# Causal attention with a row-maximum pass ahead: where the maxima's matmuls stand in each step

## The reference, cut to what matters

```
scores = jnp.einsum('bqhd,bkhd->bhqk', q, k) / jnp.sqrt(hd)
scores = jnp.where(causal, scores, -1e9)
a = jax.nn.softmax(scores, axis=-1)
out = jnp.einsum('bhqk,bkhd->bqhd', a, v).reshape(B, S, D)
```

## Time and profile before

| | us |
|---|---|
| median of 3 runs | 3145.0 (3141.05 to 3147.88) |
| profiled execution, its own time | 3123.49 |
| its span | 3122.0 |
| phase 2 in it, from the first to the last matmul | 464.9 to 2041.9 |

### The profile page before, as it was taken

How to read it: one execution, slowest core, us unless ns; L and a number is a source line. 1 busy time by engine, 2 the same in 40 slices (tenths; PEclk the granted TensorE clock), 3 DMA queues, 4 the chain that set the end, 5 groups by cost and what they waited for, 6 DMA issues and landing times. The chain is left out here.

```text
span 3122.0 us, 60368 instructions
## 1 busy us (share of the span) xinstructions
PE 2562.5 (82%) x21392; PEld 1316.3 (42%) x21392; DVE 2338.2 (75%) x3780; ACT 1543.6 (49%) x2314; POOL 2254.1 (72%) x1225
## 2 busy tenths in 40 slices
PE   7959978999999999999999999847749888999600
PEld 4524433333333333333333332236638777777500
DVE  4437758888888889888988888015657999999344
ACT  2212216677777777677777677722214444444200
POOL 4433339898889989889899998927737566566376
PEclk9979999999999999999999999968769999999855
DMA  6995542122323233232332321148667666667686
GB/s 193 200 298 180 180 162 74 46 75 81 87 55 83 79 87 86 56 80 81 86 79 63 82 72 41 30 153 254 223 198 224 202 204 205 206 205 206 215 255 198
DMA packets 346973, 435.67 MB, mean 140 GB/s; under 512 B 40858, under 2 KB 276860, under 8 KB 346748
## 3 DMA queue, kind: packets, MB, share of 16 engines
q1 hardware_dynamic: 300796, 350.81, 39.2%
q0 software_dynamic: 17920, 54.55, 5.3%
q10 hardware_dynamic: 28032, 27.27, 2.5%
HBM read 273.43 MB, written 158.47 MB: 138 GB/s over the span
## 5 line engine op out<-in xcount | busy, mean ns | idle before, releaser
L988 DVE TENSOR_REDUCE p_piece_max<-p_ring 128x1 f32<-128x512 f32 (+3 forms) x2160 | 1281.5, 653 | 180.0 <-PE p_ring L1090 97.5
L1046 ACT ACTIVATE p_probs<-p_st 128x1024 f32<-128x1024 f32 (+3 forms) x1280 | 1076.6, 894 | 445.1 <-PE p_st L1122 239.3
L1122 PE MATMUL p_st<-unit_q,unit_k 64*128 64x512 bf16 (+3 forms) x3520 | 417.9, 348 | 22.3 <-POOL p_minus_one L875 11.7
L1140 PE MATMUL p_pv<-p_probs,unit_vg 128*32 128x512 f32 (+3 forms) x3520 | 412.0, 545 | 0.0
L1749 POOL TENSOR_TENSOR p_pv<-p_pr,p_qkv 128x4096 f32<-128x4096 f32 x32 | 347.5, 10860 | 37.4 <-ACT p_pr L1847 36.8
L917 POOL TENSOR_TENSOR p_terms<-p_head_p,p_head_in 128x4096 f32<-128x4096 f32 x32 | 347.6, 10861 | 0.4
L1090 PE MATMUL p_ring<-unit_k,unit_q 64*128 64x512 bf16 (+3 forms) x1600 | 272.8, 354 | 70.1 <-DVE p_piece_max L988 69.8
L1920 PE MATMUL p_y_ps<-p_w,p_hid 128*128 128x256 f32 x1152 | 282.6, 402 | 27.6 <-ACT p_hid L1860 27.6
L896 POOL TENSOR_TENSOR p_terms<-p_head_in 128x4096 f32<-128x4096 f32 x32 | 283.0, 8843 | 8.2 <-POOL p_head_s L904 4.4
L1907 PE MATMUL p_hid_ps<-p_rT,p_w 128*128 128x256 f32 x1152 | 263.8, 382 | 2.9 <-issue 2.6
L923 POOL TENSOR_TENSOR p_terms<-p_terms 128x2048 f32<-128x2048 f32 (+2 forms) x96 | 252.6, 2632 | 17.4 <-POOL p_terms L923 11.7
(11 more groups left out here) (194 smaller groups left out, 3588.3 us busy)
## 6 DMA issues: line engine op xcount, KB each, us to landing
p_w<-ffn_w SPq DMA_DIRECT2D x144, 512.0 KB, 5.1
qk_parts<-p_parts SPq DMA_DIRECT2D x64, 384.0 KB, 3.2
head_qkv<-p_heads SPq DMA_DIRECT2D x16, 1536.0 KB, 6.7
p_rows<-sorted_rows SPq DMA_DIRECT2D x72, 256.0 KB, 4.1
expert_rows<-p_y ACTq DMA_DIRECT2D x72, 256.0 KB, 5.5
unit_q<-qk_parts SPq DMA_DIRECT2D x132, 128.0 KB, 3.2
unit_k<-qk_parts SPq DMA_DIRECT2D x132, 128.0 KB, 3.6
p_x<-attn_x SPq DMA_DIRECT2D x32, 512.0 KB, 6.9
```

The source lines that it names most:

```text
L988: nc.vector.tensor_reduce(piece_max[:, n % 2, h:h + heads, i, pc], ring_ps[g % RING][:, 0:heads * width].rearrange("p (h k) -> p h k", h=h ...
L1046: nc.scalar.activation(probs[:, 2 * turn_of(s, i) + u, :, 0:width], st_ps[u][:, :, 0:width], ACT.Exp).then_inc(probs_done, 1)
L1122: last = nc.tensor.matmul(st_ps[u][:, half, 0:width], k6[s][rows, PAIR * second + u, kt * P:(kt + 1) * P], q6[s][rows, PAIR * second + u, ...
L1140: last = nc.tensor.matmul(pv_ps[hh * VW:(hh + 1) * VW, skip:CT], vg[s][:, kt, hh * VW:(hh + 1) * VW], probs[:, 2 * turn_of(s, i) + hh % PA ...
```

## The change

`ISSUED` is no longer computed from costs. Two tables, one for unit 0 and one for all others, give three bits for each of the 40 steps. Each bit is a place in the step: behind the first `scores`, behind the second, and behind `values`. A place holds at most one pair. Unit 0 still issues 82 pairs and the others 72; the sum by step differs. VectorE's order of reductions is the same as before, apart from which of them stand ahead of its few other instructions at steps 10, 12 and 14.

```
-    def issued(n, i):
-        share = STEPS_BY[i]
-        work = share / END if n == 0 and share < END else n + 1 - END + share
-        whole = int(work + 1e-9)
-        return min(TOTAL, N_PAIR * whole + sum(by <= work - whole + 1e-9 for by in PAIRS_BY))
-    ISSUED = [[issued(n, i) for i in range(N_STEP)] for n in range(UNITS)]
+    FIRST_UNIT = """
+        101 001 011 101 010 011 011 011 111 011 011 110 100 110 100 111 011 111 111 011
+        011 111 011 011 110 101 011 111 011 101 111 011 111 011 001 011 011 011 011 001"""
+    OTHER_UNITS = """
+        100 100 010 101 011 010 011 011 011 111 011 010 011 010 010 111 011 011 011 011
+        011 011 011 011 010 101 011 011 011 011 011 011 011 011 011 011 011 010 101 001"""
+    SPOTS = [[[int(k) for k in step] for step in unit.split()] for unit in (FIRST_UNIT, OTHER_UNITS)]
+    for n in range(UNITS):
+        for i in range(N_STEP):
+            count = ISSUED[n][i] = min(TOTAL, count + sum(spots_of(n)[i]))
...
             def body(n, s):
                 for i in range(N_STEP):
+                    done = before_step(n, i)
+                    ends = [min(TOTAL, done + sum(spots_of(n)[i][:k + 1])) for k in range(3)]
                     scores(n, s, i, 0)
+                    maxima(done, ends[0])
                     scores(n, s, i, 1)
-                    done, upto = before_step(n, i), ISSUED[n][i]
-                    cut = done + (upto - done + 1) // 2
-                    maxima(done, cut)
+                    maxima(ends[0], ends[1])
                     if i >= LAG:
                         values(n, s, i - LAG)
-                    maxima(cut, upto)
+                    maxima(ends[1], ends[2])
```

More of the change, by code:

```diff
@@ L684, in phase2_attend, with spots_of @@
     LAG = 2
-    AHEAD = 6
     TOTAL = N_PAIR * (UNITS - 1)
[L688 to L693, removed]
-    def issued(n, i):
-        share = STEPS_BY[i]
-        work = share / END if n == 0 and share < END else n + 1 - END + share
-        whole = int(work + 1e-9)
-        return min(TOTAL, N_PAIR * whole + sum(by <= work - whole + 1e-9 for by in PAIRS_BY))
-    ISSUED = [[issued(n, i) for i in range(N_STEP)] for n in range(UNITS)]
-    assert all(ISSUED[n][N_STEP - AHEAD - 1] == N_PAIR * (n + 1) for n in range(UNITS - 1))
+    FIRST_UNIT = """
[5 more added lines that the diff above has]
+    SPOTS = [[[int(k) for k in step] for step in unit.split()] for unit in (FIRST_UNIT, OTHER_UNITS)]
+    assert all(len(unit) == N_STEP for unit in SPOTS)
+    def spots_of(n):
+        return SPOTS[1 if n else 0]
+    ISSUED = [[0] * N_STEP for _ in range(UNITS)]
+    count = 0
+    for n in range(UNITS):
+        for i in range(N_STEP):
+            count = ISSUED[n][i] = min(TOTAL, count + sum(spots_of(n)[i]))
+    assert all(ISSUED[n][N_STEP - 7] >= N_PAIR * (n + 1) for n in range(UNITS - 1))
     NEGATED_AT = [min(N_PAIR * u + 1, TOTAL) for u in range(1, UNITS)]
```

## The result

| | before | after |
|---|---|---|
| median of the timed runs, us | 3146.4 (3141.1 to 3149.5, 4 runs) | 3121.5 (3121.0 to 3124.7, 4 runs) |
| after / before | | 0.9925, 95% interval 0.9907 to 0.9942 |
| profiled execution: its time, its span | 3123.5, 3122.0 | 3121.0, 3119.4 |
| phase 2, from the first scores to GpSimd's first instruction of phase 3 | 465.0 to 2053.8 | 465.2 to 2031.6 |
| what lies behind it | 1068.2 | 1087.8 |

The account below looks back on a forecast made before the run. TensorE and VectorE were taken to set 98.0 us a unit, with GpSimd next at 96.5. From a median of 3145, gains of 24.0 over fourteen intervals and 2.7 from unit 0 to unit 1 gave 3118, range 3109 to 3137.

Parts of the forecast that it names:

- The first: Phase 2, fourteen intervals between GpSimd's shifts from unit 1 to 15: 1376.4 us become 1352.4, a gain of 24.0.
- The second: GpSimd's interval from unit 0 to unit 1: 103.7 us become 101.0, a gain of 2.7 (8.1 to −2.4).
- The pace of 96.5: Plain units of phase 2: GpSimd's list becomes the limit at 96.5 us, taken as 96.6 with the handshake.
- The ledger: TensorE and VectorE's loop in a plain unit: 98.0 − 4.1 − 0.4 + 0.1 = 93.6 us, taken as 94.
- the ceiling of 96: TensorE and VectorE's loop in a plain unit: at most 96 or so, if VectorE enters steps 9 to 13 behind.
- the idle time of 5.4 us given to VectorE: From unit 0 to unit 1: 5.4 us of VectorE idle added to 95.6 for 79 pairs, giving 101.0.
- the stated bound of 106.1: From unit 0 to unit 1: upper bound on the interval, 103.7 us plus two more pairs at 1.21 each.
- the cost that the prediction priced for plain units: TensorE's matmuls behind a wait for GpSimd run at half clock, about 2 us a unit, covered within 96.5.
- VectorE waiting at step 14 in each unit: VectorE's head maximum at step 14 waits for GpSimd's head scores, asked for 2.5 us early, in every unit.
- TensorE and VectorE still setting the pace: Rival, chance 0.20: short distances chain, the loop takes 97.2 us a unit, gain 15.4, time 3129.6.
- The step from the old code's three slower units to none: Units 3, 8 and 13, slowed by the clock, raise the average interval to 98.3 us; forecast 96.6 for all fourteen.
- the rival with no gain: Rival, chance 0.10: waits spread over more places are as long in sum; 3145 us, within 3.

Follow-up runs that it names:

- kernel with the tables alone: Changed kernel with new tables for unit 0 (35 pairs before step 14) and for the other units, GpSimd's list left whole; 3114.8 against 3147.8 (0.9902).
- the first experiment: Kernel before with its old count of pairs in each step, but at most one pair at a place; 3114.6 against 3127.7 (0.9952).
- both single edits: Changed kernel with only other tables (3114.8), or with only between-head sums moved to VectorE and unit 0's 33 pairs before step 14 (3108.5); each against 3147.8.
- the two together: Changed kernel with other tables, 35 pairs before step 14 in unit 0, and between-head sums and reciprocals moved from GpSimd to VectorE; 3049.5 against 3126.4 (0.9762).
- the old code with the shorter GpSimd list: Kernel before with GpSimd's reciprocal by pow replaced by a multiply, leaving out the between-head division; one run, 3120.3 us.
- the counts alone: Kernel before with the new tables' count of pairs in each step, in the two old places; 3124.2 against 3127.7 (0.9987).

## Why the prediction was right, point by point

- **The end of it.** Forecast 3118, measured 3121.5; gain 27 forecast, 24.9 measured (phase 2 ends 22.2 us earlier by the traces). The forecast came from two terms, 24.0 and 2.7. The first was right: from the second shift of unit 1 to that of unit 15 it was 1350.9 us (614.3 to 1965.2) against 1352.4 forecast and 1376.3 before, a gain of 25.4. The second had the wrong sign: −2.9. The 21.5 us between the timed runs and the trace of before, which the prediction carried over, are about the distance between the two groups (3147.8 against 3126.4 for the same kernel).
- **The pace of 96.5.** Right, in each plain unit, and GpSimd's waits vanished from them. What was wrong is the room beside it. The ledger gave the loop of TensorE and VectorE as 93.6 us and counted pairs alone; measured without GpSimd it is 96.2, just above the ceiling of 96 too. That the forecast of 96.5 held nevertheless is luck as far as the margin goes: GpSimd's list was still the longer by 0.3 us. The term that the ledger lacked is ScalarE. Steps 0, 1, 5 and 13, with one pair each, hold 1.2 to 1.6 us of TensorE's work (an estimate from its starts in the earlier trace rows), but two full exponentials take 1.94, and in steps 5 and 13 the copy of the finished block adds 0.59; halving its work there gave 94.2. The distances between pairs were priced well in sum: 93.6 against 94.2.
- **Unit 0 into unit 1.** The step that failed is the idle time of 5.4 us given to VectorE. In the stretch from 508.3 to 614.9 it was busy for 95.8 us, as worked out (95.6), but idle for 10.8; the 106.6 us lie above the stated bound of 106.1. Before, it was idle for 10.5 there (103.7 less 93.2 busy); the prediction halved this without a row that shows it, and it stayed. The new table reaches step 14 of unit 0 with two pairs fewer and earlier, waits 6.6 us for GpSimd's first head scores, and has 2.6 us more of reductions behind it. A second cost comes from the longer wait: four matmuls of scores took 1.04 us right behind it, 0.61 in the kernel before. The kernel before:

```profile
509.41 0.61 PE L1122 MATMUL p_st<-unit_q,unit_k 64*128 64x512 bf16 x4 [0.69 <-ACT p_probs L1046]
```

and the changed one:

```profile
509.05 1.04 PE L1125 MATMUL p_st<-unit_q,unit_k 64*128 64x512 bf16 x4 [6.81 <-ACT p_probs L1049]
```

The granted clock of the stretch is 0.98 where it was 1.00: the cost that the prediction priced for plain units fell due here. Unit 0 as before gave 103.3, with more pairs ahead 96.5, both at 1.00. How the 10.8 us divide between the clock and the small waits is open.

- **VectorE waiting at step 14 in each unit** didn't come; in units 1 to 14 the head maxima find GpSimd's scores ready. It is ScalarE's `head_probs` that waits for the shift, 0.2 us. With so little waiting, the clock's cost behind a long wait, put at 2 us, didn't come either in plain units: granted clock 1.00. The kernel with the tables alone shows that it would have come in some units, and that GpSimd's list would have covered it, as the prediction said.
- **The rivals.** TensorE and VectorE still setting the pace was the nearest: 0.3 us in place of 2.5 kept it from being true. The step from the old code's three slower units to none held: no unit from 1 to 13 shows a lower clock, and the longest wait at the ring in unit 5 is 0.45 us. The prediction put the lower clock down to the wait of 1.13 us alone (“only for the longest wait”); but in unit 3 of the kernel before it came twice, the first time behind a wait of 0.80 at 778.7 us, and with single pairs at a place it came in two units behind a wait of 0.70. That waits which are only spread out stay as long in sum, the rival with no gain, is nearly true of the first experiment: 0.5 us a unit.
- **"No wait at the ring above 0.8 us", "units of 96.5 to 96.7"**: as said; the longest wait for a free bank is 0.6 us, in unit 0, and units took 96.4 to 96.7. **"Under 8 us of GpSimd's idle time, nearly all in unit 1"**: 13.1, all in unit 1, by the same fault as the second term.

## What to carry to other kernels

Before pricing a schedule, list for each step what every engine of the loop needs, the one that looks idle too: ScalarE, busy for 70 us of 98, set the pace in four short steps. Where two independent chains are within a per cent of each other, an edit to one alone shows next to nothing in the units, as both single edits did here (96.5 and 96.6), and only the two together give their gain (94.1). Work of a start-up step that waits anyway for another engine is the cheapest place for anything that can be moved ahead.

## What the runs showed of the hardware

Of the units of the first trace of the kernel before, three (3, 8 and 13) show a granted clock of 0.97 to 0.98 (unit 8 in the earlier trace rows) and took 99.6 to 100.7 us instead of 98.0, though the same instruction stream with the same wait of 1.13 us stands in each plain unit. In the old code with the shorter GpSimd list it was units 2, 8 and 13 (100.8, 99.6 and 99.6 us). With the old counts and single pairs at a place, where the longest wait at the ring in a plain unit is 0.70 us, it was still two units of thirteen, 4 and 12, 99.1 us each. Unit 4 right behind that wait:

```profile
905.50 0.50 PE L1090 MATMUL p_ring<-p_k,p_q 64*128 64x384 bf16 x2 [0.70 <-DVE p_piece_max L988]
...
906.03 1.93 PE L1140 MATMUL p_pv<-p_probs,unit_vg 128*32 128x512 f32 x8
```

So with such a wait in every unit, some meet the lower clock and some don't. In the changed kernel, whose longest wait at the ring in unit 5 is 0.45 us, units 1 to 13 all show 1.00; so they do with the counts alone, whose longest in unit 5 is 0.65. With waits of 2.4 us or more of TensorE for ScalarE, in the kernel with the tables alone, five of the seven units from 1 to 13 that have one show 0.97 or 0.98.

The phases behind phase 2 took 1067 to 1073 us in nine traces and 1088 to 1095 in four, at nearly the same busy times. The four traces from one chip and the four from another are all in the lower group, the three from a third chip all in the upper. Whether it is the chip or the hour isn't shown, nor what differs. Times of two kernels that weren't taken side by side can be 20 us apart for this reason alone.
